# Projection and attention in one block, with the norm statistics on ScalarE and the first row maxima among the projection's half groups

## What is computed

```python
x = x + attn(layernorm(x), qkv_w, qkv_b, proj_w, proj_b)      # 16 heads of 16, rotary positions, causal mask
x = x + ffn(layernorm(x), centroids, ln_g, ln_b, w1, b1, w2, b2)  # each token goes to one of 8 experts
```

## Time and profile before

| | |
|---|---|
| Median of 3 runs | 979.69 us (979.33 to 980.11) |
| The profiled execution | 978.88 us |
| Its span in the profile | 976.7 us |
| Mean granted clock of PE | 0.954 |
| Projection, first instruction to the end of POOL's last part | 0 to 112 us |
| Attention | 113 to about 578 us |
| Routing and experts | the rest |

### The profile page before, as it was taken

How to read it: one execution, slowest core, us unless ns; L and a number is a source line. 1 busy time by engine, 2 the same in 40 slices (tenths; PEclk the granted TensorE clock), 3 DMA queues, 4 the chain that set the end, 5 groups by cost and what they waited for, 6 DMA issues and landing times. The chain is left out here.

```text
span 976.7 us, 20346 instructions
## 1 busy us (share of the span) xinstructions
PE 894.7 (92%) x6567; PEld 538.3 (55%) x6568; DVE 627.1 (64%) x1263; ACT 511.7 (52%) x1256; POOL 315.6 (32%) x468
## 2 busy tenths in 40 slices
PE   7999259999999999999999879981999999999996
PEld 4555013333333333333333237860999999999996
DVE  6999698888888888888888014783233333333332
ACT  1554206777778887877777853561322322322221
POOL 8999702323322332223233310353011111111111
PEclk9999658999999999999999998995999999999998
DMA  7698424222221112222231218236566566666660
GB/s 255 215 233 265 139 80 149 66 67 67 67 63 45 43 57 62 67 67 66 67 110 51 82 53 262 89 144 216 178 196 215 184 199 211 193 194 203 196 216 8
DMA packets 54890, 130.40 MB, mean 134 GB/s; under 512 B 9761, under 2 KB 30626, under 8 KB 48546
## 3 DMA queue, kind: packets, MB, share of 16 engines
q1 hardware_dynamic: 49234, 107.93, 35.7%
q0 software_dynamic: 5584, 21.54, 5.8%
HBM read 100.95 MB, written 28.48 MB: 133 GB/s over the span
## 5 line engine op out<-in xcount | busy, mean ns | idle before, releaser
L816 ACT ACTIVATE arena<-B_ps_s 128x512 f32<-128x512 f32 (+3 forms) x768 | 328.5, 494 | 121.8 <-PE B_ps_s L953 117.3
L875 DVE TENSOR_REDUCE B_block_max<-B_ps_item 128x8 f32<-128x1024 f32 x288 | 339.5, 1219 | 38.1 <-PE B_ps_item L938 34.7
L953 PE MATMUL B_ps_s<-q_stack,k_stack 99*128 99x512 bf16 (+7 forms) x768 | 190.1, 333 | 3.8 <-ACT arena L816 3.1
L797 POOL TENSOR_SCALAR_AFFINE_SELECT arena<-arena 128x256 f32<-128x256 f32 x256 | 103.9, 407 | 203.1 <-ACT arena L816 200.8
L969 PE MATMUL B_ps_o<-arena,B_v_quad 128*32 128x512 f32 (+3 forms) x1536 | 163.7, 498 | 1.0 <-ACT B_oacc L830 0.7
L953 PEld LDWEIGHTS B_ps_s<-q_stack,k_stack 99*128 99x128 bf16 (+1 forms) x768 | 54.1, 97 | 185.1 <-ACT arena L816 173.4
L1550 PEld LDWEIGHTS D_ps_h<-D_xT,arena 128*128 128x128 f32 x1248 | 148.2, 195 | 4.7 <-ACT D_xT L1488 2.8
L1550 PE MATMUL D_ps_h<-D_xT,arena 128*128 128x128 f32 x1248 | 148.7, 279 | 2.1 <-ACT D_xT L1488 2.1
L1569 PE MATMUL D_ps_y<-arena,D_hr 128*128 x624 | 141.0, 380 | 0.0
L938 PE MATMUL B_ps_item<-k_stack,q_stack 64*128 64x128 bf16 (+3 forms) x1152 | 109.0, 285 | 25.7 <-DVE B_max_of_blocks L838 13.4
L1479 ACT ACTIVATE D_hr<-D_ps_h,ffn_columns 128x128 f32<-128x128 f32 x156 | 44.5, 368 | 165.1 <-PE D_ps_h L1550 165.1
(11 more groups left out here) (143 smaller groups left out, 775.1 us busy)
## 6 DMA issues: line engine op xcount, KB each, us to landing
arena<-in_w_exp SPq DMA_DIRECT2D x39, 1024.0 KB, 5.1
qk_parts<-arena SPq DMA_DIRECT2D x32, 384.0 KB, 3.6
q_stack<-qk_parts SPq DMA_DIRECT2D x96, 128.0 KB, 2.9
rows<-payload SPq DMA_DIRECT2D x39, 257.0 KB, 2.7
arena<-in_x SPq DMA_DIRECT2D x16, 512.0 KB, 6.8
k_stack<-qk_parts SPq DMA_DIRECT2D x64, 128.0 KB, 2.9
arena<-in_w_exp POOLq DMA_DIRECT2D x8, 1024.0 KB, 6.4
...
```

Source lines behind the costliest of these rows:

```text
L797: pool.affine_select(out=block_p, in_=block_p, compare_op=ALU.is_ge, fill=0.0, base=0, pattern=[[0, 2], [1, P]], channel_multiplier=-1).th ...
L816: act.activation(pr[s % PR][:, h, 0:QW - off], ps_s[(QH * s + j) % R][:, 0:QW - off], ACT.Exp, scale=scale).then_inc(s_e, 1)
L875: dve.tensor_reduce(bmx[:, r, g:QH:GH, at:at + 4], src[:, :, :].rearrange("p c (b n) -> p c b n", n=P), AX.X, ALU.max).then_inc(s_free, 1)
L953: pe.matmul(ps_s[(QH * s + j) % R][:, 0:QW - off], ks[rows, r, half, bass.ds(g * SEQ + kb * P, P)], qs[rows, r, half, bass.ds(g * SEQ + c ...
```

## The change

- The two phases become one block, `phase_project_attend`; attention's tiles, semaphores and instruction streams follow the projection's without a boundary. The projection's PSUM for the values and the scale is now the second item tile, that of q and k is later the scores' and the output's.
- The statistics of a token go from DVE (`bn_stats`, `bn_aggr`) to ACT: a Copy with scale -1/256 whose accumulated output is the negative mean, and a Square with that as bias, whose accumulated output is the sum of squares. They stand behind the second part and ahead of the root.
- 11 of the 18 items of the first quad are written and reduced in half groups 9 to 15 (`AHEAD`), all in the first item tile, so that each waits for the reduce of the one before. The last of each half group stands behind the values on PE and behind the normalization on DVE, another one ahead of the values and ahead of the rest. The other 7 follow the loop, two of them ahead of the last rest on DVE.
- The block maxima lie in 8 x 8 slots for each head, preset once, so that one reduce and one copy combine them. Four items have 4 blocks of one row, two have 2 + 2, one has 4 single blocks (before: 1, 2, 1, 2, 1, 2, 1 parts of the seven).
- The casts of the masks go to ACT and come before the loop, the preset of the value tile to POOL's start. The bias product of the values goes to h = 4. The split of that bias on POOL goes to step 1 (from 0), its rows on SP to step 2 (from 1), and the first four loads of expert weights on POOL to steps 1 and 2 (from 0 and 1).
- The third stack is loaded in the projection's loop (h = 13 to 16) and no longer at step 0 of attention.
- The weights, the rotary tables and the constants of the projection go into the large shared tile; the exponentials of attention reuse their place, so the first ones wait for the projection's last parts.

```diff
-            phase_project(...)
-            phase_attention(...)
+            phase_project_attend(...)
...
-        wq = sb("wq", [P, DC, 3 * DIM])
-        rp = sb("rope_tab", [P, 2, SEQ])
-        st = sb("st", [P, 2, TG, 6])
+        wq = take("early", 1, DC * 3 * DIM)[:, 0, :].rearrange("p (c n) -> p c n", c=DC)
+        rp = take("early", 1, 2 * SEQ)[:, 0, :].rearrange("p (a n) -> p a n", a=2)
+        junk = take("early", 1, DIM)[:, 0, :].bitcast(BF16).rearrange("p (a n) -> p a n", a=2)
...
+        ps_qk = [ps(f"ps_pair{i}", [P, 2, QW]) for i in range(2)]
+        ps_i = [ps(f"ps_item{i}", [P, 2, QW]) for i in range(2)]
+        ps_v = ps_i[1][:, 0, :].rearrange("p (a n) -> p a n", a=2)
+        ps_bc = ps_i[1][:, 1, :]
+        ps_s = [ps_qk[0][:, 0, :], ps_qk[0][:, 1, :], ps_qk[1][:, 0, :]]
+        ps_o = ps_qk[1][:, 1, :]
...
+        banks = [[(t, 0, 4, 0)] for t in range(4, KB)]
+        slots = [(KB * t + 1, 2) for t in range(4, KB)]
+        for t in (2, 6):
+            banks.append([(t, t - 2, 2, 0), (t + 1, t - 2, 2, 2)])
+            slots.append((KB * t, 4))
+        banks.append([(2 * u + 1, 2 * u, 1, u) for u in range(4)])
+        slots.append((KB + 6, 2 * KB))
...
+        AHEAD = {9: (0,), 10: (1, 2), 11: (3,), 12: (4, 5), 13: (6,), 14: (7, 8), 15: (9, 10)}
+        DRAIN = 11
-        early_at = (0, 0, 1, 1, 14, 14, 15, 15)
+        early_at = (1, 1, 2, 2, 14, 14, 15, 15)
```

```diff
-                    if 5 <= h < 9:
-                        load_stack(sp, Step(0), ..., range(4 * (h - 5), 4 * (h - 4)))
-                    if 9 <= h < 13:
-                        load_stack(sp, Step(1), ..., range(4 * (h - 9), 4 * (h - 8)))
+                    if h >= 5:
+                        Q, part = divmod(h - 5, 4)
+                        load_stack(sp, Step(Q), ..., range(4 * part, 4 * part + 4))
```

ScalarE:

```diff
                 def root(g):
                     if g < NG:
-                        act.wait_ge(s_var, TG * (g + 1))
-                        act.activation(sd[:, g % 4, 0, :], mv[:, g % 2, :, 1], ACT.Sqrt, bias=eps).then_inc(s_sd, 1)
+                        act.wait_ge(s_sq, TG * (g + 1))
+                        act.activation(sd[:, g % 4, 0, :], mv[:, g % 2, :, 1], ACT.Sqrt, bias=eps, scale=1.0 / DIM).then_inc(s_sd, 1)
+
+                def stats(t):
+                    g, i = t // TG, t % TG
+                    if g < NG:
+                        if i == 0:
+                            act.wait_ge(s_x[g % XR], 16 * (g // XR + 1))
+                            if g >= 2:
+                                act.wait_ge(s_sd, g - 1)
+                        act.activation(junk[:, 0, :], xt[:, g % XR, i, :], ACT.Copy, scale=-1.0 / DIM,
+                                       accum_out=mv[:, g % 2, i, 0:1]).then_inc(s_mean, 1)
+                        act.wait_ge(s_mean, t + 1)
+                        act.activation(junk[:, 1, :], xt[:, g % XR, i, :], ACT.Square, bias=mv[:, g % 2, i, 0:1],
+                                       accum_out=mv[:, g % 2, i, 1:2]).then_inc(s_sq, 1)
...
-                root(0)
-                root(1)
+                for g in range(2):
+                    for t in range(TG * g, TG * (g + 1)):
+                        stats(t)
+                    root(g)
+                act.wait_ge(s_cr, 16)
+                act.activation(ml[:, :, :], ..., ACT.Copy).then_inc(s_ones, 1)
+                act.activation(mr[:, :, :], ..., ACT.Copy).then_inc(s_ones, 1)
                 for h in range(NH + 1):
...
                         act.activation(parts(m, 1), res[:, m % 2, :, :], ACT.Copy).then_inc(s_p2, 1)
+                    if h < NH:
+                        for t in (2 * h + 2 * TG, 2 * h + 2 * TG + 1):
+                            stats(t)
                     if h % 2 == 1:
                         root(h // 2 + 2)
+
+                act.wait_ge(s_p3, NH)
```

VectorE, in the loop over half groups and behind it:

```diff
+                    if h == 4:
+                        add_value_bias(dve, ps_v[:, 0, :])
+                    for item in AHEAD.get(h, ())[:-1]:
+                        reduce_item(Step(-1), item)
+                    if h == NH:
+                        for item in range(DRAIN, DRAIN + 2):
+                            reduce_item(Step(-1), item)
                     if m >= 0:
...
                     if h < NH and h % 2 == 0:
                         normalize(h // 2 + 1)
-                    if h < NH:
-                        t = 2 * h + 2 * TG
-                        for u in range(2):
-                            stats(t + u)
-                        variances(t, t + 2)
+                    for item in AHEAD.get(h, ())[-1:]:
+                        reduce_item(Step(-1), item)
+                for item in range(DRAIN + 2, UNITS):
+                    reduce_item(Step(-1), item)
```

In `reduce_item` the combination behind the last item of a step is now:

```diff
-                                for t in order:
-                                    dve.tensor_reduce(mo[:, r, :, t], ...)
-                                for half in range(2):
-                                    dve.tensor_tensor(mx[:, r, half, :, :]..., ALU.max)
+                            dve.tensor_reduce(mo[:, :], bmx[:, :, :].rearrange("p h (t b) -> p (h t) b", t=KB),
+                                              AX.X, ALU.max).then_inc(s_mc, 1)
+                            wait(dve, s_mc, Q, 2, 1)
+                            dve.tensor_copy(mx[:, :, :, :], mo[:, :]...).then_inc(s_mc, 1)
```

TensorE, in the loop over half groups and behind it:

```diff
+                    if h == min(AHEAD):
+                        pe.wait_ge(s_ones, 2)
+                        pe.wait_ge(s_fix, 4)
+                    for item in AHEAD.get(h, ())[:-1]:
+                        put_item(Step(-1), item)
+                    if h == 4:
+                        pe.wait_ge(s_v, 2 * h)
+                        value_bias(pe, ps_v[:, 0, :])
+                        pe.wait_ge(s_bw, 2)
                     values(2 * h, 2 * h + 2)
+                    for item in AHEAD.get(h, ())[-1:]:
+                        put_item(Step(-1), item)
                     if h % 2 == 0:
                         spread(g + 1)
...
+                pe.wait_ge(s_z, NG)
+                for item in range(DRAIN, UNITS):
+                    put_item(Step(-1), item)
```

704 lines of the change are left out of this document (326 added, 378 removed).

## The result

The changed kernel takes 990.37 us (median of 4 runs, 990.23 to 992.24) where the kernel before takes 979.51 on the same chip (4 runs, 978.44 to 980.11): a ratio of 1.0117 (of the means; 95% interval 1.0099 to 1.0134), or 11.5 us slower; the medians lie 10.9 apart. The forecast was 984.9, slower by 5.2. The profiled execution took 990.51 us, its span is 988.8.

The account below looks back on a forecast made before the run. The prediction took PE to bound attention and POOL to set the projection's pace. Its terms, 2.8 + 9.7 + 16.7 - 24.0 = +5.2 us on 978.88, gave 984.1, and 0.8 for the median 984.9 us; range 976.5 to 993.

Parts of the forecast that it names:

- S: ACT's cost for the statistics of a half group's two tiles: 2.3 us, bounded between 1.5 and 3.2.
- r: The start of rest 8 on DVE in the projection, from which the forecast counted later times.
- The start, +2.8: Before the loop, statistics on ACT with one table load: root done at 11.05 against 8.26, 2.8 us later.
- (a): Rival, chance 0.17: the accumulated output on ACT is free, S = 1.8, time 980 us.
- (b): Rival, chance 0.23: the loop on ACT is short; at S = 1.5 the median is 976.9 us.
- (c): Rival, chance 0.14: ACT is slower still, S = 3.2, time 994 us.
- Half groups 1 to 8, +9.7: Projection: ACT's statistics close a loop, a pair takes 13.8 us instead of 11.4, four pairs cost 9.7 us more.
- Item 0: Half group 9: PE's first item waits for the stack, landing at r + 6.1; products 10 end at r + 13.2.
- The eleven items, +16.7: Half groups 9 to 15: items among DVE's work, last products at r + 47.7, 16.7 us more than before.
- The tail, -24.0: From the last product to the first maxima: 14.3 us left on DVE instead of 38.3, 24.0 less.
- rival (d): Chance 0.04: PE's clock falls to 1.2 GHz in the projection, 9 us a pair over four pairs, 1021 us.
- At nothing: Parts said to cost nothing: new banks, shorter combination under PE in attention, bias split, later expert loads.

Follow-up runs that it names:

- one_table: The changed kernel with one square root of eps on ACT ahead of its wait for x: 1.0085 of the kernel before.
- bias_early_add: The changed kernel with DVE's add of the value bias moved ahead of half group 4's reciprocal and products: 1.0062 of the kernel before.
- vector_bias_stack: The changed kernel with statistics back on DVE, the bias add at the head of half group 4, first stack's loads in half groups 5 and 6: 0.9859 of kernel before.
- stats_behind_values: The changed kernel with ACT's statistics moved from behind the second part to ahead of it, behind the values: 1.0058 of the kernel before.

## Why the prediction was right or wrong

The sign and the loop through ACT were right; the size was less than half of what came (5.2 for 10.9 in the medians, 11.5 by the ratio). Two steps failed: the half groups, where the add of the value bias was in no term (5.4 us), and the eleven items, whose matmuls were said to lie beside DVE's work (3.4 us). In the table above the start is off by +0.8, the loop by -2.9, the bias add by +5.4, the items by +3.4 and the tail by -1.0, which is the 5.7 us between 5.2 and 10.9: a part of the errors cancelled. That the time lies in the range (976.5 to 993.0) is luck. The range was made from S and the stack's landing, and with S = 2.07 and the landing at r + 5.8 it gives a time below the forecast; what carried the time towards its upper end was a term that it did not hold. Step by step:

- *The start, +2.8.* Measured +3.6. S was too high (2.07 for 2.3), which is 0.5 less in two pairs of tiles, and "I take one load, as before" was wrong: two loads, 1.28 more. The first half of that sentence had the right bound, and nothing in the trace of before spoke for the value that I took. one_table shows the whole.
- *S = 2.3.* The Copy 0.40 and the Square 0.51 were as forecast, the sum's output 0.19 and not 0.13: the row that I called nearest (0.198) was the price itself. The Square starts 0.04 behind the end of the Copy's read, for 0.05. The tile is nevertheless 1.03 and not 1.15: its four instructions add up to 1.29, but three starts in each tile lie about 0.1 ahead of the end of what is before them, where the forecast had one such overlap of 0.05. By the forecast's own 1 us for each 0.1 of S this would have made 982.6, further from the result. Rivals (a) and (b), at S = 1.8 and 1.5, are out, and so is (c) at 3.2, though its 994 was near.
- *Half groups 1 to 8, +9.7.* The loop is there: the pair from rest 5 to rest 7 takes 13.08 us, and 9.2 + 2 S with S = 2.07 gives 13.3. Four of those are 52.3 us, 6.8 more than the 45.5 of before, where the forecast had 9.7. The other 5.4 us are half group 4. This is the step that failed, by omission: the part on the statistics went through each instruction of the loop but the moved bias product of h = 4 and its add, which are in no term and in no list of what costs nothing. The forecast gave the reciprocal a wait for the root in every even h from 2 on; the add stands two places behind it on DVE, and PE's values stand behind the add. Following that wait down DVE's queue would have found it. bias_early_add shows 5.3 us by rest 8 and 5.4 by the time.
- *Item 0.* Forecast: the stack lands at r + 6.1, products 10 end at r + 13.2. Measured from rest 8 = 85.29: the item at r + 5.8, the products at r + 13.7. Right, with the granted clock of 0.73 for the 0.72 that I gave that chain; the 0.5 us more are a third product behind PE's second chain, where the sum has room for two. But PE was idle for 6.17 us ahead of it and not for 9: "its values of h = 9 (1.8) wait only for ACT's of h = 8" left out PE's spread of half group 8, which waited 2.49 us for the reciprocal, and the slow chains behind it. The landing decided, so this cost nothing.
- *The eleven items, +16.7.* Measured +20.1. Up to the end of products 12 the forecast is right: r + 28.8 for 28.7, the 0.5 of the item before being taken up by the wait for the root. Products 13 then end 1.9 us late, products 14 another 0.5 and products 15 another 1.0. The step that failed is "PE's items (0.3 each) lie beside this DVE work". An item on PE waits for a reduce that stands behind DVE's products, and DVE's next products wait for the chains behind that item, as PE's timeline of the changed kernel shows:

```profile
126.86 0.39 PE L884 MATMUL ps_item<-k_stack,q_stack 64*128 64x512 bf16 x2
127.18 1.99 PE L832 MATMUL ps_item<-arena 128*128 128x256 f32 x8
130.22 0.39 PE L884 MATMUL ps_item<-k_stack,q_stack 64*128 64x256 bf16 x4 [1.05 <-DVE B_block_max L748]
130.54 3.70 PE L910 MATMUL ps_pair<-arena 128*128 128x512 f32 x8
134.17 0.39 PE L884 MATMUL ps_item<-k_stack,q_stack 64*128 64x256 bf16 x4
```

All eleven items have one PSUM tile. The item that starts at 130.22 waits for the reduce of the one before; that reduce stands on DVE behind the products, three of them (2.07) behind the end of PE's second chain; and the next chains stand behind the item. Item 0.3, two chains 3.65, three products 2.0, a reduce 1.2 and handovers make 7.3 us, the measured distance of rests 13 and 14 (130.08, 137.40); the forecast had 6.3 from the end of products 14 to that of products 15, counted on DVE alone. Every version with these items has that distance, with the stack early or late and the statistics on either engine (104.84 to 112.16 in vector_bias_stack). A second tile for them was not tried. The 1.9 us ahead of products 13 are mostly the clock behind such a wait, below.
- *The tail, -24.0.* Measured -25.0. But it was the forecast's one gain, and I did not split it. The runs do: of the 24.5 us by which the stretch from rest 15 to the first score shrank (42.5 to 18.0), 11.0 are the block boundary, for which the half groups pay nothing, and 13.5 the items, for which rests 8 to 15 take 15.7 us longer (56.8 for 41.1).
- *The clock, rival (d).* Not at half speed over four pairs, as (d) had it, but in pieces behind PE's waits, which the windows of the changed kernel show:

```profile
56.00:77.00 21.00, 18.85 (x63) 11.00 (x61) 12.59 (x17) 14.94 (x40) 17.11 (x10) 1.00 0.71 206
...
77.00:82.00 5.00, 4.55 (x10) 2.47 (x11) 4.79 (x7) 2.67 (x5) 3.17 (x2) 0.66 0.83 245
...
115.00:120.00 5.00, 4.72 (x12) 2.51 (x13) 4.24 (x5) 2.00 (x2) 2.56 (x2) 0.66 0.27 70
```

PE had waited 2.49 us ahead of 77.45 and 2.82 ahead of 115.28; the chains behind them took 4.99 and 4.52 us, where 3.60 and 3.70 are usual. What such a fall costs depends on the place. The first cost nothing: rests 7 and 8 are 5.35 us apart, as they are in bias_early_add. The second held products 13 up: item, spread and chains took 5.97 us there and 4.41 from 100.13 on, and rests 11 and 12 are 8.13 apart, against 6.57 in stats_behind_values, where PE waits 1.90 us at that place and the clock behind it is 1.00. Nor does the length of the wait decide alone. In the changed kernel and in bias_early_add PE waits equally long in half group 8:

```profile
77.45 0.98 PE L821 MATMUL ps_item<-cst,A_sd 128*128 128x128 f32 x4 [2.49 <-DVE A_sd L702]
78.23 4.99 PE L910 MATMUL ps_pair<-arena 128*128 128x512 f32 x8
```

```profile
72.13 0.65 PE L821 MATMUL ps_item<-cst,A_sd 128*128 128x128 f32 x4 [2.50 <-DVE A_sd L702]
72.62 3.60 PE L910 MATMUL ps_pair<-arena 128*128 128x512 f32 x8
```

In the second the clock stays at 1.00, and in stats_behind_values it does so behind a wait of 3.37 us at 46.65. What makes the difference was not found. In vector_bias_stack the clock is 1.00 from 70 to 113 us.
- *At nothing.* Right to 0.8 us for attention and its new banks (432.5 us for 431.7), and right for the 10.45 us to the first score.

The Trainium skill (ScalarE activation tables: per-element evaluation and per-set limits, What a function is on this engine) says that the accumulator output works the same whichever table is read, and that with the same operands the instruction costs the same. The rows agree as far as they go: the output costs 187 ns behind a Copy (L623) and 186 behind a Square (L626). They show besides that it is read by an instruction of its own. The Trainium skill's rule to batch activations by table set (ScalarE: Activation LUTs, Table sets: the hidden batching unit) is about one load or two; here the order decides too: the Copy had a table loaded for it when it came first, and the Sqrt then another; behind the Sqrt's load the Copies and Squares needed none.
